# Rope tables from 16 rows through TensorE, norms ahead of the rope, and three score units moved into the first head

## The reference, cut to what matters

```
h = layernorm(x) * (1 + ca) + sa          # ca, sa: rows of silu(c) @ wmod
q = rope(h @ Wq.T)   # 32 heads of 16
k = rope(h @ Wk.T)   # 8 heads of 16
v = h @ Wv.T         # 8 heads of 16
x = x + ga * (softmax(causal(q k^T / 4)) v) @ Wo.T
rope(t) = t * cos + rotate_half(t) * sin  # cos, sin: 1024 tokens x 16
```

## Time and profile before

| | before |
|---|---|
| runs (median, lowest, highest) | 758.24, 757.90, 758.73 us |
| span of the profiled execution | 756.9 us |
| median less that span | 1.3 us |
| PE busy | 713.5 us (94%) |
| DVE busy | 474.8 us (63%) |
| mean granted TensorE clock | 0.986 |
| share of the chain that ended last | PE 76%, DVE 12%, issue 5% |

### The profile page before, as it was taken

How to read it: one execution, slowest core, us unless ns; L and a number is a source line. 1 busy time by engine, 2 the same in 40 slices (tenths; PEclk the granted TensorE clock), 3 DMA queues, 4 the chain that set the end, 5 groups by cost and what they waited for, 6 DMA issues and landing times.

```text
span 756.9 us, 10266 instructions
## 1 busy us (share of the span) xinstructions
PE 713.5 (94%) x3718; PEld 431.1 (57%) x3718; DVE 474.8 (63%) x716; ACT 318.3 (42%) x536; POOL 314.5 (42%) x254
## 2 busy tenths in 40 slices
PE   4998899999999999889999999999789999999998
PEld 2444334333333332258788888554358788877886
DVE  3787677888888885237765558768895433338211
ACT  3311267677767767751335310554234223223100
POOL 0325673756565574861456233115431222125300
PEclk9999799999999999999999999999889999999999
DMA  8357516263251200230023100213010111111111
GB/s 307 107 126 220 124 43 164 73 123 54 72 123 26 30 3 29 75 113 14 29 62 105 56 1 0 78 50 66 1 68 1 57 55 39 44 55 57 42 69 42
DMA packets 24111, 53.00 MB, mean 70 GB/s; under 512 B 4252, under 2 KB 8100, under 8 KB 23044
## 3 DMA queue, kind: packets, MB, share of 16 engines
q1 hardware_dynamic: 24068, 52.44, 25.0%
HBM read 45.63 MB, written 6.60 MB: 69 GB/s over the span
## 4 chain that ended last, share of the span: by engine, by line
PE 76%; DVE 12%; issue 5%; DMA 2%; ACT 2%; SPq 2%; POOL 1%; DVEq 0%; ACTq 0%; POOLq 0%
PE ps L867 73%; DVE mxp L1810 2%; DMA rq<-in_mask 1%; DVE st L1652 1%; PE ps L884 1%; DVE xnb L1676 1%; ACT pr L1456 1%; DVE x L2007 1%; PE ps L1051 1%; DVE rt L1691 1%; DVE x L1894 1%; PE ps L1119 0%; DVE dg L2041 0%; SPq L717 0%; DVE qsw L1861 0%
## 5 line engine op out<-in xcount | busy, mean ns | idle before, releaser
L867 PE MATMUL ps<-arena 128*128 128x512 f32 (+1 forms) x1404 | 325.9, 392 | 1.4 <-DVE arena L1695 0.7
L867 PEld LDWEIGHTS ps<-arena 128*128 128x128 f32 (+1 forms) x1404 | 259.6, 186 | 59.3 <-DVE arena L1695 1.4
L1810 DVE TENSOR_REDUCE mxp<-ps 128x2 f32<-128x1024 f32 (+3 forms) x160 | 172.8, 1115 | 44.5 <-PE ps L867 43.9
L1456 ACT ACTIVATE pr<-ps 128x512 f32<-128x512 f32 x288 | 162.1, 596 | 75.7 <-PE ps L867 71.9
L867 PE MATMUL ps<-Qst,Kst 99*128 99x512 bf16 x288 | 100.2, 389 | 6.1 <-ACT pr L1456 4.8
L867 PE MATMUL ps<-Kst,Qst 96*128 96x512 bf16 (+3 forms) x384 | 98.6, 334 | 5.4 <-DVE mxp L1810 4.2
L2248 POOL TENSOR_TENSOR pr<-pr,cap 128x512 int32<-128x512 int32 x56 | 71.1, 1285 | 38.3 <-ACT pr L1456 38.3
L867 PE MATMUL ps<-pr,vr 128*32 128x512 f32 x576 | 76.5, 604 | 0.0
L867 PEld LDWEIGHTS ps<-Qst,Kst 99*128 99x128 bf16 x288 | 24.5, 98 | 79.7 <-ACT pr L1456 63.9
L867 PEld LDWEIGHTS ps<-Kst,Qst 96*128 96x128 bf16 x384 | 36.4, 99 | 51.3 <-DVE mxp L1810 20.2
L2347 POOL TENSOR_TENSOR arena<-raw,arena 128x1024 fp32r<-128x1024 f32 x11 | 26.7, 2431 | 80.2 <-ACT arena L1530 80.2
(11 more groups left out here) (203 smaller groups left out, 822.2 us busy)
## 6 DMA issues: line engine op xcount, KB each, us to landing
wmr<-in_wmr SPq DMA_DIRECT2D x8, 1280.0 KB, 11.0
raw<-in_w SPq DMA_DIRECT2D x16, 512.0 KB, 3.3
Qst<-q_parts SPq DMA_DIRECT2D x42, 128.0 KB
q_parts<-qparts SPq DMA_DIRECT2D x3, 768.0 KB, 5.0
x<-in_x SPq DMA_DIRECT2D x8, 256.0 KB, 6.0
wm<-in_wm SPq DMA_DIRECT2D x4, 512.0 KB, 7.5
raw<-in_up SPq DMA_DIRECT2D x8, 256.0 KB, 2.6
raw<-in_down SPq DMA_DIRECT2D x8, 256.0 KB, 2.6
```

The source lines that it names most:

```text
L867: return nc.tensor.matmul(outp, lhs, rhs, start=start, stop=stop, skip_group_check=True)
L1456: A(pr[:, k % PRING, :], ps[:, 4 + k % 2, :], ACT.Exp, scale=float(DH) ** -0.5).then_inc(exp_done, 1)
L1810: V.tensor_reduce(mxp[:, kh, g0:g0 + heads, i].rearrange("p (b e) -> p b e", e=per), units, AXX, ALU.max)\
```

## The change

The 16 distinct rows of cos and sin are loaded ahead of x, with a 16 by 128 selection matrix made from the identity, and PE spreads them to 128 partitions by 4 matmuls; ACT copies the 4 banks to SBUF. On DVE the norm of half 1 comes whole before the rope, and the mask is cast between rope_begin(0) and rope_end(0) (from rq3). On PE values(0) goes from before ln_turn(0,1) to the end of the opening, and queries(1,0) goes from there into the fills, which are now 12 halves. Of head 1's six units ahead, three stay and three go to slots 0, 1, 2 of the first head's body.

```diff
+    for k in range(4):
+        banks.add(("trig", k), bank=4 + k)
-FILL = (("q", 1, 1), ("v", 1), ("q", 2, 0), ("q", 2, 1), ("q", 3, 0))
+FILL = (("q", 1, 0), ("q", 1, 1), ("v", 1), ("q", 2, 0), ("q", 2, 1), ("q", 3, 0))
-FILL_AT = (0, 1, 3, 5, 7, 9, 11, 14, 17, 19)
-VT_AT = 8
+FILL_AT = (0, 1, 2, 3, 5, 6, 8, 10, 12, 14, 17, 19)
+VT_AT = 7
+BEGUN = 3
+BEGUN_AT = (0, 1, 2)
...
+    if not ctx:
+        todo += [(BEGUN_AT[s - BEGUN], "s", 1, s) for s in range(BEGUN, AHEAD)]
...
             sp.dma_start(cols[:, 0:18], a["cols"]).then_inc(c_in, 16)
+            sp.dma_start(sel16[:, :].rearrange("p (h d) -> p h d", d=DH),
+                         a["ident"][0:DH, 0:DH].unsqueeze(1).to_broadcast([DH, NKV, DH])).then_inc(trig_in, 16)
+            sp.dma_start(trig16[:, 0:T], a["cos"][0:DH, :]).then_inc(trig_in, 16)
+            sp.dma_start(trig16[:, T:2 * T], a["sin"][0:DH, :]).then_inc(trig_in, 16)
...
-            sp.dma_start(rq[0][:, 0:2 * P], a["mask"]).then_inc(mask_in, 16)
+            sp.dma_start(rq[3][:, 0:2 * P], a["mask"]).then_inc(mask_in, 16)
-            for hf in range(2):
-                sp.dma_start(cosb[:, tok[hf]], a["cos"][:, tok[hf]]).then_inc(trig_in[hf], 16)
-                sp.dma_start(sinb[:, tok[hf]], a["sin"][:, tok[hf]]).then_inc(trig_in[hf], 16)
...
+            pe.wait_ge(trig_in, 48)
+            for k in range(4):
+                b = bank_of(pe, ("trig", k))
+                mm(ps[:, b, :], sel16[:, :], trig16[:, HALF * k:HALF * k + HALF], True, True).then_inc(full_b[b], 1)
             pe.wait_ge(c_silu, 1)
...
             queries(0, 0)
-            values(0)
             ln_turn(0, 1)
             keys(1)
             queries(0, 1)
-            queries(1, 0)
+            values(0)
...
-            for s in range(AHEAD):
+            for s in range(BEGUN):
                 if s < 2:
                     queries(3, 1, range(2 * s, 2 * s + 2))
                 s_unit(1, s)
...
+            for k in range(4):
+                b = filled(act, ("trig", k))
+                A(trigb[:, k // 2, tok[k % 2]], ps[:, b, :], ACT.Copy).then_inc(read_b[b], 1)
             act.wait_ge(consts, 2)
...
             first_modulation()
-            dve.wait_ge(mask_in, 16)
-            V.tensor_copy(maskb[:, :, :].rearrange("p a b -> p (a b)"), rq[0][:, 0:2 * P]).then_inc(k_ones, 1)
-            V.tensor_scalar(cap[:, :], rq[0][:, P:2 * P], 0.0, None, ALU.is_ge).then_inc(cap_ready, 1)
             dve.wait_ge(x_in[1], 64)
             for t in range(4):
                 ln_stat(1, t)
             ln_finish(0, 1)
-            dve.wait_ge(k_ones, 2)
-            dve.wait_ge(cap_ready, 1)
-            dve.wait_ge(trig_in[0], 32)
+            ln_norm(0, 1)
+            evacuated(dve, ("trig", 0))
             rope_begin(0)
-            ln_norm(0, 1, range(2))
+            dve.wait_ge(mask_in, 16)
+            V.tensor_copy(maskb[:, :, :].rearrange("p a b -> p (a b)"), rq[3][:, 0:2 * P]).then_inc(k_ones, 1)
+            V.tensor_scalar(cap[:, :], rq[3][:, P:2 * P], 0.0, None, ALU.is_ge).then_inc(cap_ready, 1)
             rope_end(0)
-            ln_norm(0, 1, range(2, 4))
             key_rest(0)
...
-                    if n == 0 and k == 2:
+                    if n == 0 and k == 5:
                         swap_queries(3)
...
-            for s in range(AHEAD):
+            for s in range(BEGUN):
                 s_unit(1, s)
-                if s == AHEAD // 2 - 1:
+                if s == 1:
                     swap_queries(2)
```

More of the change, by code:

```diff
@@ L312, in ctx_at @@
     return slots_before(n + 2, "ctx")
-FILL = (("q", 1, 1), ("v", 1), ("q", 2, 0), ("q", 2, 1), ("q", 3, 0))
+FILL = (("q", 1, 0), ("q", 1, 1), ("v", 1), ("q", 2, 0), ("q", 2, 1), ("q", 3, 0))
 FILL_HALVES = [(job, range(2 * h, 2 * h + 2)) for job in FILL for h in range(2)]
-FILL_AT = (0, 1, 3, 5, 7, 9, 11, 14, 17, 19)
-VT_AT = 8
-assert len(FILL_AT) == len(FILL_HALVES) and FILL_AT[3] < VT_AT and FILL_AT[-1] < NS
+FILL_AT = (0, 1, 2, 3, 5, 6, 8, 10, 12, 14, 17, 19)
+VT_AT = 7
+assert len(FILL_AT) == len(FILL_HALVES) and FILL_AT[5] < VT_AT and FILL_AT[-1] < NS
 MOD_BY_PE = 3
@@ L326 @@
 AHEAD_AT = (26, 29, 29, 31, 33, 34)
+BEGUN = 3
+BEGUN_AT = (0, 1, 2)
+assert BEGUN + len(BEGUN_AT) == AHEAD
 assert len(SCORES_AT) == NS - AHEAD and len(AHEAD_AT) == AHEAD
@@ L447, in adaln_two_blocks @@
         wq = at("wq", [P, KC, D], F32, ACT_B + 56 * 1024)
-        cosb = at("cosb", [P, T], F32, WR_B + 32 * 1024)
-        sinb = at("sinb", [P, T], F32, WR_B + 36 * 1024)
+        trigb = at("trigb", [P, 2, T], F32, WR_B + 32 * 1024)
+        cosb, sinb = trigb[:, 0, :], trigb[:, 1, :]
+        trig16 = at("trig16", [DH, 2 * T], F32, WR_B + 40 * 1024)
+        sel16 = at("sel16", [DH, P], F32, HT_B + 29 * 1024)
         rsw = at("rsw", [P, 4, HALF], F32, HT_B)
@@ L565, in adaln_two_blocks @@
         wm0_in = [sem(f"mod0_weights{kc}_loaded") for kc in range(KC)]
-        trig_in = [sem(f"cos_sin{hf}_loaded") for hf in range(2)]
+        trig_in = sem("trig_rows_loaded")
         c_in, ident_in, mask_in = (sem(n) for n in
@@ L1078, in _ @@
                 pe.wait_ge(read_b[b], banks.attn[b])
-            pe.wait_ge(k_ones, 1)
+            pe.wait_ge(k_ones, 2)
             pe.wait_ge(kst_ones, 1)
@@ L1793, in _ @@
             query_parts(0)
-            dve.wait_ge(trig_in[1], 32)
+            evacuated(dve, ("trig", 1))
             rope_begin(2)
             rope_end(2)
+            dve.wait_ge(k_ones, 2)
+            dve.wait_ge(cap_ready, 1)
             rope_begin(3)
@@ L2190, in _ @@
             for hf in range(2):
-                pool.wait_ge(trig_in[hf], 32)
+                evacuated(pool, ("trig", hf))
+                evacuated(pool, ("trig", 2 + hf))
                 sines(2 * hf)
@@ L2201, in rope_queries @@
                 pool.wait_ge(q_raw, 2 * c)
-                link(nc.gpsimd.tensor_tensor(qacc[:, :], qraw[c - 1], cosb[:, :], ALU.mult))
+                link(nc.gpsimd.tensor_tensor(qacc[:, :], qraw[c - 1], cosb, ALU.mult))
                 pool.wait_ge(sw_done, 2 * c)
-                link(nc.gpsimd.tensor_tensor(qsw[c - 1], qsw[c - 1], sinb[:, :], ALU.mult))
+                link(nc.gpsimd.tensor_tensor(qsw[c - 1], qsw[c - 1], sinb, ALU.mult))
                 link(nc.gpsimd.tensor_tensor(qacc[:, :], qacc[:, :], qsw[c - 1], ALU.add))
```

## The result

| | before | after |
|---|---|---|
| median of 16 runs each, taken in turn | 757.74 us | 759.76 us |
| lowest and highest | 754.56, 759.11 | 758.50, 761.31 |
| span of the profiled execution | 756.9 us | 757.1 us |
| mean granted clock of it | 0.986 | 0.991 |

After against before the ratio is 1.0032, interval 1.0022 to 1.0042: slower by 2.4 us (the two medians differ by 2.0), and 759.8 lies 0.5 us above the forecast of 759.3. The two spans hardly differ (0.2 us), so one profile of each would have said "no change". The profiled execution of before was one of its slower ones, that of after one of its faster ones: it took 758.87 us, the second shortest of 16. In every profile with a device time of its own that time is about 1.8 us above the span (here 758.87 for 757.1).

A forecast was written before the change was run, and what follows sets the result against it. PE was taken as the bound (76% of the chain), DVE at the first body's start. Opening -0.2, score stretch +2.0, first body -0.7 made +1.1: span 758.0, median 759.3 us; own range 758.2 to 760.4, full range 756.4 to 761.6.

The forecast's parts named there:

- the score stretch: Score units of head 0, PE-bound: queries(1,0) moved into it makes 33.1 us against 31.09, loss 2.0 us.
- the opening: Up to the first score matmul: mask and table waits leave DVE, x half 1 comes later; gain 0.2 us.
- the first body: From max_turn(0) to max_turn(1): three units moved behind t_units 0 to 2, slow clock expected again; gain 0.7 us.
- The count of passes (48 against 40): Score stretch: PE has 48 passes, 20.9 us, instead of 40, 17.4 us; with the other 11.4, 32.3 us.
- the 0.8 us of idle that was left room for: Score stretch: of the present 2.2 us of PE idle, 0.8 was expected to remain, giving 33.1 us.
- The four table matmuls: Opening, on PE before the first modulation matmul: 8 passes of 0.44 us, 3.5 us, costed at nothing.
- The casts of the mask, costed at nothing: Opening, on DVE: half a microsecond, expected to lie in the wait for GpSimd's sine product.
- these 2.0 contain the end of the slow clock: First body: 34.1 against 36.1 us would gain 2.0, but the clock was expected to fall again, losing 1.5.
- Slow clock gone: Rival, first body: the three units fill PE's hole enough to keep 2.4 GHz; 757.8 us, chance 0.22.
- Opening wins more: Rival, opening: x half 1 not late, landing at 17.1, key_rest 2.0 us earlier; 757.5 or 756.5 us, chance 0.13.
- The PE-bound stretch pays all: Rival, score units of head 0: no idle absorbed, +3.5 us; 760.8, or 762.0 with the worse opening; chance 0.23.
- a stretch at 0.50 in PE's new hole near 29: Opening, sign of being wrong: granted clock at 0.50 in the hole that values(0) leaves on PE.

The follow-up runs named there:

- Fills_alone: The kernel before with only the new order of projections and the 12 fill halves on PE; 759.58 us, ratio 1.0040.
- six_ahead: The changed kernel with all six units of head 1 ahead of the first body, as before the change; 759.85 us, ratio 1.0034.
- fills_back: The changed kernel with values(0), queries(1,0) and the fills back in their old places; 758.01 us, ratio 1.0020.
- Opening_filler: The kernel before with the change's opening alone, plus unread matmuls (4, 1, 6) ahead of head 1's units 3 to 5; 756.76 us, ratio 0.9990.
- filler: The kernel before with 11 unread bf16 matmuls (4, 1, 6) ahead of units 3, 4 and 5 of head 1; 755.44 us, ratio 0.9977.
- opening_only: The changed kernel with old fills, PE order and units, so only the change's opening is left; 758.61 us, ratio 1.0018.
- order_turn: The kernel before with the new DVE order, mask from rq3, values(0) behind ln_turn(0,1), tables still loaded whole; 755.73 us, ratio 0.9984.
- middle group: 37 of 94 runs of the kernel before, unchanged, told by a mean granted clock of 0.991; 756.9 us in the mean.
- after_filler: The changed kernel with unread matmuls ahead of head 1's units 3 to 7 and in the hole near 29; 759.68 us, ratio 1.0029.
- after_again: The changed kernel measured and profiled once more, nothing changed; 759.27 us, ratio 1.0031 to the kernel before.

## Why the prediction was right or wrong

The time came out as forecast, 759.8 for 759.3, and within the forecast's own range. That is luck in part: the change itself was forecast at +1.1 us and measured at 2.0 by the medians and 2.4 by the ratio, about twice as much. Of its three terms the score stretch holds in place and size, the opening in place, and the first body does not hold.

**The score stretch, +2.0: right.** It was 33.1 and is 33.22, +2.13, in every kernel with the new fills, and 31.1 (31.56 once) in every kernel without them. The count of passes (48 against 40) and the 0.8 us of idle that was left room for both hold: PE is idle for 1.13. Fills_alone shows that this move alone makes a loss of this size. In the place it came from, queries(1,0) had cost nothing.

**The opening, -0.2: near, with two sizes off.** DVE did wait for x half 1, no more for the mask, in five of seven profiles (in six_ahead and fills_back it waits for neither); the shuffle of rope_begin(0) came at 25.37 and 25.02 in the two profiles of the new kernel for a forecast of 25.0, F at 43.0 for 42.6. (The working shows 3.6 us from the shuffle to key_rest(0) and adds 3.7; it took 3.76.) The x stream was shifted by 1.7 to 2.25 us as DVE saw it (half 0 read from 8.23 to 8.77 in seven profiles, 6.52), where I took 1.4 from the issues and 2.2 as the bound; x's first issue itself moved by 1.38 (1.18 to 2.56), so the remaining 0.3 to 0.9 is in the transfers. The Trainium skill, SBUF — State Buffer, "Door 1: The DMA port swizzle", gave 1.3 us of estimate on top for so few partitions; these profiles agree with its sign and show a quarter to two thirds of the size, and nothing tells it from other causes. The four table matmuls took 7.19 us, twice the 3.5 us forecast; the 0.44 us a pass had been read from a later stretch, and PE ran its first work at half that pace. The first modulation matmul came right behind them, at 11.52 instead of 9.97 in the kernel before, yet the chain of waits does not touch PE there: it goes from x's last load (issued at 10.42, 8.87 us long) into DVE. The casts of the mask, costed at nothing, took 1.12 + 0.2 us and ended 0.3 us behind the product that was to hide them.

In the marks the seven profiles with the new opening have F at 42.84 in the mean, the five with the old one 42.57: +0.3. The runs say more. Opening_filler stands 1.2 us above filler, opening_only 1.3 above before, each give or take about 1. What makes up the rest was not found: the runs of opening_only fall in a group around 756.6 and one around 759.0 at nearly the same mean clock, and in opening_filler the clock also fell for 3.4 us near 330, in a part of the kernel that the change leaves alone. In fills_back and order_turn_filler it fell there too. This stays open.

**The first body, -0.7: wrong in its reason.** I compared with 36.1 us, and took that for the kernel. It is the kernel at a slow clock, which by the mean clock some 4 runs in 10 have: at full clock the same body takes 33.3. The three runs shown with the profile (757.9 to 758.7) lie at that level too (758.3, above); over 110 runs in all the medians of the kernel before were 756.6 to 757.7. Against the mixture of the two, 0.38 x 36.2 + 0.62 x 33.3 = 34.4, the spread units at 34.65 lose 0.25, and against an undisturbed body they lose 1.35. If the 1.5 us of the middle group lay in this body as well, the mixture would be 35.0 and they would gain 0.35. So the term is near nothing, as six_ahead says too. The step that failed is "these 2.0 contain the end of the slow clock": the clock was counted into the gain as if it always fell. The rest of that step, that moving PE's units wins little there, held: unit 8 was read 16.4 us behind max_turn(0), for 17.1. But from there the forecast had 17.0 us at full clock to the next max_turn, and after_filler, at full clock, took 18.3. What I left out was GpSimd's chain, which moved together with the shuffles that I had listed.

Put together from the marks, 0.3 + 2.1 + 0.25 = +2.7 us, against 2.4 measured. That this closes proves little: the runs with the filler give 1.2 for the opening and 2.4 for the fills, and 4.1 for the whole change above filler. That leaves 0.5 for the spread units, where the marks say 1.3, again give or take about 1. The prediction had +1.1 on a base of 758.2, which was 0.5 us above the 757.74 that the kernel before then had beside the new one: the change was sized 0.9 us too small and the base 0.5 us too high, and the two nearly cancel.

**The rivals.** "Slow clock gone" fell: with the clock held up by a filler, the new kernel still took 759.68. So, with nm held up beside GpSimd, a clock that stays up gained nothing there. "Opening wins more" fell: x was late, and the shuffle started at 25.37, not at 23.2. "The PE-bound stretch pays all" fell in its mechanism, as idle was absorbed (1.13 left of 2.2 us), though the measured time is close to its 760.8. (The rivals' own ends, 756.5 and 762.0, are not quite those of the range, 756.4 and 761.6; nothing here hangs on that.) The named sign of being wrong, a stretch at 0.50 in PE's new hole near 29, came in some executions (after_again, mean 0.66 over 5 us, not in the first profile), and cost nothing that F shows. The Trainium skill, TensorE: Matmul & The Clock Gate, "A second HAM failure mode: psum-queue depth-cycling", was cited against thin spreading; here the stretch was shorter in the three profiles with spread units and no filler (6.8, 6.8 and 3.4 us) than in the two of the kernel before (10.2). So these traces don't bear that use out; but it varies by execution (0 to 10.2 us with the units unspread), and so few profiles don't show the opposite either.

## What to carry to other kernels

Before a gain is taken from a stretch at low clock, see in how many runs that stretch occurs: one profile shows one kind. The mean granted clock of each run shows that there are several kinds, though not where each one's slow stretch lies. Work that PE does while it waits for something is free only there; eight passes moved into a stretch where PE is the bound cost their time less the idle that they can fill. And where PE idles ahead of a PE-bound stretch, a few unread matmuls were worth 1.7 us in the kernel before, more than any part of the change gained; in the kernel after they were worth nothing.

## What the runs showed of the hardware

- The same 4.06 us with PE busy 1.55 or 1.56 us stand in six profiles with the units unspread and no filler. The granted clock was 0.50 behind them for 10.2 us in three, for 3.4 us in one, and not at all in two; with PE busy 3.92 us there it did not fall. The 10.2 us cost 2.9 us between two marks (36.2 for 33.3), the 3.4 us only 0.2 (33.50).
- A float32 matmul with 16 rows of contraction and 512 columns ran at 0.90 us a pass (7.19/8) at a recorded clock of 1.00, where the passes of 128 rows ran at 0.44. That is the pace of 1.2 GHz, and the 16 rows need not be the reason: 8 transposes over all 128 rows took 1.92 us at 18.41 in fills_back and 1.04 us at 16.91 in opening_only, both at a recorded clock of 1.00. So in the first 20 us the recorded clock did not tell PE's pace. A 16-row matmul at a later time was not run.
- Small DVE operations from SBUF to SBUF end with the GpSimd operation that they meet: nm took 0.19 us alone, and 0.68, 1.00, 1.04 and 1.78 beside the last product, each time until 0.04 to 0.05 us behind its end; a cast of the mask took 1.12 instead of 0.29. The reductions from PSUM kept their 1.2 us each.
